# An expert layer whose slots fetch their own token rows: an indirect gather beside each indirect return

## The chip, the cores and the metric

The kernel runs on one core of one Trainium2 chip. The metric is the device time of one execution in microseconds (us). Before the change it is 2861.53 us, the median of three runs that lie between 2859.42 and 2862.87 us.

## The reference, cut to what matters

The kernel computes a nonlocal block, an attention layer with three branches, and a layer of eight experts, over 4 x 1024 tokens of 128 channels. Only the last layer is touched:

```python
m = jnp.mean(x, -1); xn = (x - m) / sqrt(var + eps)   # layer norm of 4096 tokens x 128
logits = xn @ router_w.T                              # 8 experts
probs = softmax(logits); p2, i2 = top_k(probs, 2)     # two experts a token
p2 = p2 / (sum(p2) + 1e-9)
h = silu(xn @ w1[e].T) * (xn @ w3[e].T)               # 341 hidden units
y = h @ w2[e].T                                       # back to 128 channels
out = x + sum over the two chosen e of p2[e] * y[e]
```

The 4096 tokens give 8192 pairs of token and expert. Pairs are sorted by expert into slots of 128 rows. Each expert is padded to whole slots, so that 64 + 7 = 71 slots always suffice.

## The kernel before, in words

Three stages run one behind the other, each closed by a barrier of all engines: the heads, the attention, and the experts (`experts_part`). The last has two blocks with a barrier between them.

`route_block` loads the tokens, turns them (PE, L1569; ACT, L1594), normalizes them into `xe[0]` (DVE, L1648), turns them back for the router (PE, L1577; ACT, L1602), multiplies by the router (PE, L1582) and takes softmax, ranks and the position of each pair among the slots (DVE, L1653 to L1704). Meanwhile SP clears the 9088 rows of `xs` in DRAM (L1555): each row has 128 values and one word, the number of the pair, which starts out of range. POOL makes a second copy `xe[1]` of the rows (L1620). When `where` is there (L1704), POOL issues 64 indirect DMAs (L1627), two for each tile of 128 tokens, which scatter the rows with their pair numbers to their places in `xs`. It waits until all have landed. DVE works out the gates and the owner (the expert) of each slot (L1707 to L1713). ACT rounds the three weight tensors to a high part (L1607, L1608), and DVE subtracts it to get the low part (L1716, L1719).

`experts_block` runs over the 71 slots. SP loads groups of `GROUP` = 4 slots from `xs` into one of three buffers of `xin` (L1764). A load waits for the returns of the group that had the buffer before. PE runs, in step i: `hidden(i)` (six matmuls, L1802 to L1807); in every fourth step, where i % 4 is 1, `turn_x(i // 4 + 1)`, four transposes of the next group (L1789); then `turn_h(i - 1)` (L1816) and `output(i - 2)` (L1826, L1828). ACT and DVE follow in the same order: silu, split of x and of h, and `result(i - 2)`, a copy and an addition into one of four buffers `y` (L1924, L1926). For each slot POOL waits for that result and issues one indirect DMA (L1894) that returns the 128 rows to their places in `ys`; the row numbers are the word beside each row of `xin`. At the end SP loads `ys` in order (L1773), DVE adds with the gates, and PE, ACT and SP turn and store.

All instructions of an engine run in the order of the code. A wait stands in that order and holds all that is behind it.

Of the kernel before, what the change touches and what calls it, by code (L numbers as in the profile page):

```python
# [8 lines left out]
F32 = mybir.dt.float32  # L9
# [6 lines left out]
P = 128  # L16
# [1464 lines left out]
ROW = P + 1  # L1481
GROUP = 4
LAST_ROWS = HIDP - (KH - 1) * P
# [3 lines left out]
def experts_part(nc, d, t2_dram, out, ps, ident, eps, sb, kept):  # L1487

    m = Mem()
    m.ps, m.ident, m.eps = ps, ident, eps
    m.xs = kept("xs", (SLOTS * P, ROW))
    m.ys = kept("ys", (2 * B * T, C))
    m.w1 = [sb(n, [C, NE, HIDP], F32R) for n in ("w1h", "w1l")]
    m.w3 = [sb(n, [C, NE, HIDP], F32R) for n in ("w3h", "w3l")]
    m.w2 = sb("w2hl", [P, NE, KH, 2, C], F32R)
    m.t_tok = sb("t_tok", [P, TILES_OF, P])
    m.gate = sb("gate_of", [P, 2, TILES_OF])  # L1500
    m.owner = sb("owner", [P, SLOTS], I32)
    with ExitStack() as mem:
        route_block(nc, m, d, t2_dram, lambda *a: mem.enter_context(nc.sbuf_tensor(*a)))
    experts_block(nc, m, out, sb)


def route_block(nc, m, d, t2_dram, sb):
# [3 lines left out]
    raw = [sb(n, [P, x], F32) for n, x in (("raw_w1", NE * HIDP), ("raw_w3", NE * HIDP), ("raw_w2", NE * KH * C))]  # L1511
    t2 = sb("t2_all", [C, B, T], F32)
    xe = [sb("xe%d" % k, [P, TILES_OF, ROW], F32) for k in range(2)]
    xf = t2[:].rearrange("c b t -> c (b t)")
    empty = sb("empty", [P, ROW], F32)
# [4 lines left out]
    token = sb("token", [P, 2, TILES_OF], I32)  # L1520
# [12 lines left out]
    slot = sb("slot", [P, 2, TILES_OF], F32)  # L1533
    where = sb("where", [P, 2, TILES_OF], I32)
    owner_f = sb("owner_f", [P, SLOTS], F32)
    stack = ExitStack()
    s = open_sems(nc, stack, "w_loaded t_loaded0 t_loaded1 t_loaded2 t_loaded3 small_loaded empty_set cleared w_hi "
                             "turned t_copied stats aggregated std_done xn_done back back_copied logits_done shifted "
                             "exp_done chosen_done counted placed scattered chain id_done copied ones_set")
# [3 lines left out]
    with nc.Block() as block:  # L1543
        @block.sync
        def _(sp):
            for b in range(B):
                sp.dma_start(t2[:, b, :], t2_dram[b]).then_inc(s["t_loaded%d" % b], 16)
            small = ((router, "router"), (tie, "tie"), (before, "before"), (token, "token"), (steps, "steps"),
                     (places, "places"))
            for dst, name in small:  # L1550
                sp.dma_start(dst[:], d[name]).then_inc(s["small_loaded"], 16)
            for k, name in enumerate(("w1", "w3", "w2")):
                sp.dma_start(raw[k][:], d[name]).then_inc(s["w_loaded"], 16)
            sp.wait_ge(s["empty_set"], 2)
            sp.dma_start(m.xs.rearrange("(i p) n -> p i n", p=P),  # L1555
                         empty[:].unsqueeze(1).to_broadcast([P, SLOTS, ROW])).then_inc(s["cleared"], 16)
            sp.wait_ge(s["cleared"], 16)
# [4 lines left out]
        def _(pe):  # L1562
# [9 lines left out]
            for g in range(groups):  # L1572
# [3 lines left out]
                for i in range(GROUP):  # L1576
                    mm = pe.transpose(ps[:, 2 + g % 2, i * P:(i + 1) * P], xe[0][:, GROUP * g + i, 0:P], m.ident[:])  # L1577
                mm.then_inc(s["back"], 1)
            pe.wait_ge(s["small_loaded"], 16 * 6)
            for t in range(TILES_OF):  # L1580
# [7 lines left out]
                .then_inc(s["counted"], 1)  # L1588

        @block.scalar  # L1590
        def _(act):
# [13 lines left out]
            act.wait_ge(s["w_loaded"], 48)  # L1605
            for k, (hi, lo) in enumerate((m.w1, m.w3)):
                act.copy(hi[:].rearrange("p e n -> p (e n)"), raw[k][:]).then_inc(s["w_hi"], 1)  # L1607
            act.copy(m.w2[:, :, :, 0, :], raw[2][:].rearrange("p (e k n) -> p e k n", e=NE, k=KH)).then_inc(s["w_hi"], 1)  # L1608

        @block.gpsimd  # L1610
        def _(pool):
            pool.memset(empty[:, 0:P], 0.0).then_inc(s["empty_set"], 1)
            pool.memset(empty[:, P:ROW].bitcast(I32), 2 * B * T).then_inc(s["empty_set"], 1)
            pool.wait_ge(s["small_loaded"], 16 * 6)
            for k in range(2):
                pool.tensor_copy(xe[k][:, :, P].bitcast(I32), token[:, k, :]).then_inc(s["id_done"], 1)
            for g in range(groups):
                gg = slice(GROUP * g, GROUP * (g + 1))
                pool.wait_ge(s["xn_done"], GROUP * (g + 1))
                pool.tensor_copy(xe[1][:, gg, 0:P], xe[0][:, gg, 0:P]).then_inc(s["copied"], 1)  # L1620
            pool.wait_ge(s["cleared"], 16)
            pool.wait_ge(s["id_done"], 2)
            pool.wait_ge(s["copied"], groups)
            pool.wait_ge(s["placed"], 1)
            for t in range(TILES_OF):
                for k in range(2):
                    pool.indirect_dma_start(m.xs, bass.IndirectOffsetOnAxis(ap=where[:, k, t:t + 1], axis=0),  # L1627
                                            xe[k][:, t, :], None, bounds_check=SLOTS * P - 1, oob_is_err=False)\
                        .then_inc(s["scattered"], 16)
            pool.wait_ge(s["scattered"], 16 * PAIRS_OF)  # L1630

        @block.vector
        def _(dve):
# [9 lines left out]
            for b in range(B):  # L1643
# [3 lines left out]
                for t in range(NT * b, NT * (b + 1)):  # L1647
                    dve.tensor_scalar(xe[0][:, t, 0:P], m.t_tok[:, t, :], mv[:, t, 0:1], rstd[:, t:t + 1], ALU.subtract,  # L1648
# [16 lines left out]
            dve.wait_ge(s["small_loaded"], 16 * 6)  # L1665
# [35 lines left out]
            for k in range(2):  # L1701
                run(dve.tensor_tensor(picked[k], chosen[:, k], pos[:], ALU.mult))
                run(dve.tensor_reduce(slot[:, k, :], picked[k], AX, ALU.add))
            dve.tensor_copy(where[:], slot[:]).then_inc(s["placed"], 1)  # L1704
# [9 lines left out]
            for k, (hi, lo) in enumerate((m.w1, m.w3)):  # L1714
                dve.wait_ge(s["w_hi"], k + 1)
                dve.tensor_tensor(lo[:].rearrange("p e n -> p (e n)"), raw[k][:],  # L1716
                                  hi[:].rearrange("p e n -> p (e n)").bitcast(F32), ALU.subtract)
            dve.wait_ge(s["w_hi"], 3)
            dve.tensor_tensor(m.w2[:, :, :, 1, :], raw[2][:].rearrange("p (e k n) -> p e k n", e=NE, k=KH),  # L1719
                              m.w2[:, :, :, 0, :].bitcast(F32), ALU.subtract)  # L1720
# [4 lines left out]
def experts_block(nc, m, out, sb):  # L1725
# [4 lines left out]
    m.xin = sb("xin", [P, 3, GROUP, ROW])  # L1730
# [6 lines left out]
    m.y = sb("y_out", [P, 4, C])  # L1737
# [5 lines left out]
                             "hi_done lo_done y_ready y_done put0 put1 put2 put3 got0 got1 got2 got3 got4 got5 got6 got7 half_done added out_ready "  # L1743
# [6 lines left out]

    def puts_before(i, k):

        return len(range(k, i, 4))

    with nc.Block() as block:
        @block.sync
        def _(sp):
            for g in range(loads):
                if g >= 3:
                    last = tiles(g - 3)[-1]  # L1760
                    for k in range(4):
                        sp.wait_ge(s["put%d" % k], 16 * puts_before(last + 1, k))
                n = len(tiles(g))
                sp.dma_start(m.xin[:, g % 3, 0:n, :],  # L1764
                             m.xs[GROUP * g * P:(GROUP * g + n) * P].rearrange("(i p) n -> p i n", p=P))\
                    .then_inc(s["in%d" % (g % 3)], 16)
            for k in range(4):
# [15 lines left out]
        def _(pe):  # L1783
            def turn_x(g):
                pe.wait_ge(s["in%d" % (g % 3)], 16 * (g // 3 + 1))
                if g > 0:
                    pe.wait_ge(s["xl_done"], g)
                for i in range(len(tiles(g))):
                    mm = pe.transpose(ps[:, 7, i * P:(i + 1) * P], m.xin[:, g % 3, i, 0:P], m.ident[:])  # L1789
# [99 lines left out]
        def _(pool):  # L1889
            for i in range(SLOTS):  # L1890
                g = i // GROUP
# [133 lines left out]
```

## Time and profile before

| | |
|---|---|
| median of three runs | 2861.53 us |
| profiled execution, its own time | 2860.51 us |
| its span, first to last instruction | 2858.6 us |
| PE busy over the span | 2337.6 us (82%) |
| DVE busy | 1682.3 us (59%) |
| ACT busy | 1215.4 us (43%) |
| POOL busy | 537.8 us (19%) |
| route block, about | 2473 to 2636 us |
| experts block, about | 2636 to 2858 us |

How to read it: the stages follow one another, so that the busy shares of the whole span say little of this change. It lies wholly behind 2473 us, and there each stage has another engine that works. The page also has the span in 40 slices of 71.5 us each, in which PE is busy for 2 tenths of slice 36 and for less than one of slice 37. DMA records give the time from issue to landing. The granted clock is the clock at which TensorE was let run, in shares of 2.4 GHz: 0.50 is 1.2 GHz and 1.00 is 2.4 GHz. A time in brackets behind an instruction is the idle time of its engine before it, and the arrow names what ended it.

### The profile page before, as it was taken

What the parts mean: (1) busy time and instruction counts of PE and PEld (TensorE: products, weight loads), DVE (VectorE), ACT (ScalarE), POOL (GpSimd) and SP (SyncE); (2) the same over time, 40 slices, a digit from 0 to 9 for tenths busy, and PEclk for the clock granted to TensorE, in tenths of its full rate; (3) what the DMA queues carried; (4) which work ended last, traced back from release to release, by engine and by line L of the source; (5) the groups of instructions that cost most, each with busy time, mean ns of one, the idle gap of its engine ahead of it and who ended that gap; (6) DMA issues with size and microseconds to landing.
All of it is one profiled execution on the core that took longest, in us unless ns stands there. A gap on an engine that the chain in (4) does not pass through costs nothing. (4 is left out here: it accounts for less than half of the span.)

```text
span 2858.6 us, 46600 instructions
## 1 busy us (share of the span) xinstructions
PE 2337.6 (82%) x16656; PEld 1554.2 (54%) x16656; DVE 1682.3 (59%) x3155; ACT 1215.4 (43%) x2665; POOL 537.8 (19%) x575
## 2 busy tenths in 40 slices
PE   5585867763899999799999799999899999620995
PEld 3354545542566666466566466666566665310884
DVE  4767676764366566366566365665465664550676
ACT  2343333430455555355455355555355555410442
POOL 0133333352011011011011010110010110235332
PEclk8787887885999999899999899999899999755997
DMA  2254545478647546455655465565466461431113
GB/s 94 99 212 164 189 182 196 171 284 204 138 96 145 126 97 138 106 126 109 127 125 119 91 132 125 114 130 117 105 139 125 97 145 37 127 58 52 46 52 108
DMA packets 222862, 360.74 MB, mean 126 GB/s; under 512 B 68794, under 2 KB 124701, under 8 KB 222240
## 3 DMA queue, kind: packets, MB, share of 16 engines
q1 hardware_dynamic: 218304, 349.20, 48.8%
q0 software_dynamic: 4320, 8.43, 0.9%
q8 instruction: 141, 2.31, 0.4%
q14 instruction: 97, 0.79, 0.1%
HBM read 229.58 MB, written 126.56 MB: 125 GB/s over the span
## 5 line engine op out<-in xcount | busy, mean ns | idle before, releaser
L1400 ACT ACTIVATE prob<-ps 128x512 f32<-128x512 f32 (+5 forms) x1600 | 636.5, 441 | 733.5 <-PE ps L1351 587.7
L1453 DVE TENSOR_REDUCE maxima<-ps 128x1 f32<-128x512 f32 (+3 forms) x768 | 387.7, 547 | 293.7 <-PE ps L1279 146.5
L1372 PE MATMUL ps<-prob,plain 128*32 128x512 f32 (+5 forms) x3200 | 512.0, 443 | 0.0
L1423 POOL TENSOR_TENSOR products<-products,sums 128x256 f32<-128x256 f32 x192 | 140.3, 731 | 1604.5 <-DVE sums L1444 1603.2
L1458 DVE TENSOR_REDUCE maxima<-ps 128x2 f32<-128x512 f32 (+1 forms) x512 | 294.2, 608 | 242.9 <-PE ps L1290 99.7
L1444 DVE RECIPROCAL sums<-sums 128x256 f32<-128x256 f32 x192 | 331.5, 1736 | 103.9 <-ACT sums L1411 103.9
L1343 PE MATMUL ps<-q1a_s,k1a_s 128*128 128x512 f32 (+3 forms) x768 | 303.4, 395 | 0.0
L1351 PE MATMUL ps<-q1b_s,k1b_s 128*128 128x512 f32 (+3 forms) x768 | 301.3, 393 | 0.0
L1372 PE MATMUL ps<-prob,v_s 128*32 128x512 f32 (+3 forms) x1536 | 284.4, 491 | 0.0
L1279 PE MATMUL ps<-k1a_s,q1a_s 128*128 128x512 f32 (+3 forms) x768 | 234.4, 375 | 2.8 <-DMA k1a_s<-k1ah_dram 2.8
L1343 PEld LDWEIGHTS ps<-q1a_s,k1a_s 128*128 128x128 f32 x768 | 147.4, 192 | 126.8 <-issue 118.9
L1409 ACT ACTIVATE products<-ps,gates_a 64x512 f32<-64x512 f32 x192 | 131.0, 682 | 194.6 <-PE ps L1372 194.5
L1343 PE MATMUL ps<-qa_s,kwa_s 128*128 128x192 f32 (+2 forms) x576 | 175.2, 304 | 19.5 <-ACT prob L1400 15.9
L1351 PE MATMUL ps<-qb_s,kwb_s 128*128 128x192 f32 (+2 forms) x576 | 184.2, 323 | 0.0
L1343 PEld LDWEIGHTS ps<-qa_s,kwa_s 128*128 128x128 f32 x576 | 110.0, 191 | 98.2 <-issue 65.6
L932 POOL TENSOR_TENSOR rope<-turned 128x512 f32<-128x512 f32 (+1 forms) x80 | 93.5, 1168 | 353.5 <-DVE turned L959 350.5
L1279 PEld LDWEIGHTS ps<-k1a_s,q1a_s 128*128 128x128 f32 x768 | 145.8, 197 | 20.8 <-DVE maxima L1453 8.1
L1351 PEld LDWEIGHTS ps<-q1b_s,k1b_s 128*128 128x128 f32 x768 | 151.7, 198 | 5.4
L1298 PE MATMUL ps<-kwa_s,qa_s 128*128 128x192 f32 x512 | 124.8, 326 | 33.9 <-DMA kwa_s<-kwh_dram 33.9
L1372 PEld LDWEIGHTS ps<-prob,plain 128*32 128x32 f32 x3200 | 147.7, 109 | 0.0
L914 ACT CAST pairs<-ps 128x512 fp32r<-128x512 f32 (+1 forms) x112 | 62.2, 555 | 197.5 <-PE ps L888 115.8
L1343 PE MATMUL ps<-qa_s,ksa_s 128*128 128x512 f32 x256 | 114.2, 446 | 37.3 <-issue 18.9
(332 smaller groups left out, 4837.1 us busy)
## 6 DMA issues: line engine op xcount, KB each, us to landing
qh_dram<-pairs SPq DMA_DIRECT2D x96, 512.0 KB, 3.3
kwh_dram<-pairs SPq DMA_DIRECT2D x64, 512.0 KB, 3.0
qa_s<-qh_dram SPq DMA_DIRECT2D x128, 256.0 KB, 4.5
kwa_s<-kwh_dram SPq DMA_DIRECT2D x128, 256.0 KB, 7.4
q1a_s<-qh_dram SPq DMA_DIRECT2D x128, 256.0 KB, 4.7
qb_s<-qh_dram SPq DMA_DIRECT2D x64, 256.0 KB, 9.0
kwb_s<-kwh_dram SPq DMA_DIRECT2D x64, 256.0 KB, 9.9
k1a_s<-k1ah_dram SPq DMA_DIRECT2D x32, 512.0 KB, 6.9
```

The source lines that it names most:

```text
L932: pool.tensor_tensor(m.rope[:, j % 2, 0:w], m.turned[:, j % 2, 0, 0:w], m.turned[:, j % 2, 1, 0:w], ALU.add).then_inc(s["added"], 1)
L1279: mm = pe.matmul(bank[:, 0:k1 - k0], m.q1a[:, k, h, i * P:(i + 1) * P], m.k1a[:, k, k0:k1], start=True, stop=True)
L1298: pe.matmul(bank[:, i * KEEP:i * KEEP + WN], m.qa[:, k, h, t * P:(t + 1) * P], m.kwa[:, k, h, k0:k0 + WN], start=True, stop=True, skip_gro ...
L1343: pe.matmul(bank, kx, qx[:, k, h, q0:q0 + w], start=True, stop=False, skip_group_check=True)
L1351: pe.matmul(bank, ky, qy[:, k, h, q0:q0 + w], start=False, stop=True, skip_group_check=True)\
L1372: mm = pe.matmul(ps[at:at + VD, SCORES + k % 2, q0 - c * CH:q0 - c * CH + w], w_, m.prob[:, n % PROBS, h, 0:w], start=first, stop=True, sk ...
L1400: act.activation(m.prob[:, u % PROBS, h, 0:w], ps[:, turn % SCORES, 0:w], ACT.Exp, scale=SCALE).then_inc(s["exp_done"], 1)
L1409: act.activation(m.products[rows, br, cc], ps[0:NW, SCORES + k % 2, :], ACT.Copy, scale=m.gates[0:NW, br:br + 1])
L1423: pool.tensor_tensor(o, o, m.sums[:, br, cc], ALU.mult).then_inc(s["divided"], 1)
L1444: dve.reciprocal(total, total).then_inc(s["inverse_done"], 1)
L1453: ins = dve.tensor_reduce(partial[:, h, i, part:part + 1], bank[:, 0:w], AX, ALU.max)
L1458: ins = dve.tensor_reduce(negs[1 if kind == "max1" else 2][:, at:at + 2], bank.rearrange("p (i n) -> p i n", i=2)[:, :, 0:w], AX, ALU.max, ...
```

## The change

- `xs` now holds the 4096 normalized rows in token order. SP stores them in eight DMAs of 256 KB as they get ready. The clearing, the second copy `xe[1]` and the 64 scatters are gone.
- The inverse of the placement (which pair lies in lane p of slot s) is computed. For 64 tiles of pairs, DVE makes a bf16 one-hot matrix of the lane of each pair (`at_lane`, four parts of 128x2048 elements) and a mask of the slot edges behind it (`marks`, 128x4608 elements, once compared and once multiplied by the tile's number; ACT makes a copy scaled by the token's lane). PE multiplies 64 times, one-hot (128x128) by marks (128x144), and sums in one bank. DVE turns the sums into `get` (row to fetch) and `put` (row to return to) with ten small operations.
- The high parts of w1 and w3 are rounded by ACT in the midst of its copies back, behind groups 1 and 3. The low parts are subtracted on POOL, no longer on DVE.
- In the experts block SP loads no rows. POOL fetches each slot with an indirect DMA (`get`), eight before the loop and then one ahead of each return. There are eight `y` buffers instead of four. The load of a group counts as landed when all its slots have.

```diff
-    m.xs = kept("xs", (SLOTS * P, ROW))
+    m.xs = kept("xs", (B * T, P))
@@ route_block, PE
+            for q in range(QUARTERS):
+                pe.wait_ge(s["lanes_done"], q + 1)
+                pe.wait_ge(s["behind_done"], 2)
+                pe.wait_ge(s["named_done"], 1)
+                for n in range(q * PAIRS_OF // QUARTERS, (q + 1) * PAIRS_OF // QUARTERS):
+                    mm = pe.matmul(ps[:, 7, 0:2 * EDGES], at_lane[:, n, :], marks[:, n].rearrange("p a s -> p (a s)"),
+                                   start=n == 0, stop=n == PAIRS_OF - 1)
+            mm.then_inc(s["found_done"], 1)
@@ route_block, ACT
                 act.copy(xf[:, g * CH:(g + 1) * CH], ps[:, 2 + g % 2, :]).then_inc(s["back_copied"], 1)
+                if g == 1:
+                    act.wait_ge(s["w_loaded"], 48)
+                if g in (1, 3):
+                    k = g // 2
+                    act.copy((m.w1, m.w3)[k][0][:].rearrange("p e n -> p (e n)"), raw[k]).then_inc(s["w_hi"], 1)
@@ route_block, POOL
-            for t in range(TILES_OF):
-                for k in range(2):
-                    pool.indirect_dma_start(m.xs, bass.IndirectOffsetOnAxis(ap=where[:, k, t:t + 1], axis=0),
-                                            xe[k][:, t, :], None, bounds_check=SLOTS * P - 1, oob_is_err=False)\
-                        .then_inc(s["scattered"], 16)
-            pool.wait_ge(s["scattered"], 16 * PAIRS_OF)
+            for k, (hi, lo) in enumerate((m.w1, m.w3)):
+                pool.wait_ge(s["w_hi"], k + 1)
+                pool.tensor_tensor(lo[:].rearrange("p e n -> p (e n)"), raw[k],
+                                   hi[:].rearrange("p e n -> p (e n)").bitcast(F32), ALU.subtract).then_inc(s["w_lo"], 1)
+            pool.wait_ge(s["w_hi"], 3)
+            pool.tensor_tensor(m.w2[:, :, :, 1, :], raw[2].rearrange("p (e k n) -> p e k n", e=NE, k=KH),
+                               m.w2[:, :, :, 0, :].bitcast(F32), ALU.subtract).then_inc(s["w_lo"], 1)
@@ route_block, DVE, in place of the cast to where
+            run(dve.tensor_copy(slot_i[:], slot[:]))
+            run(dve.tensor_scalar(lane_i[:], slot_i[:], P - 1, None, ALU.bitwise_and))
+            run(dve.tensor_copy(lane[:], lane_i[:]))
+            dve.wait_ge(s["w_lo"], 2)
+            dve.tensor_tensor(marks[:, :, 0, :], each_tile(slot[:], EDGES), each_token(edges[:], PAIRS_OF), ALU.is_ge)\
+                .then_inc(s["behind_done"], 1)
+            n = PAIRS_OF // QUARTERS
+            for q in range(QUARTERS):
+                qq = slice(q * n, (q + 1) * n)
+                dve.tensor_tensor(at_lane[:, qq, :], each_tile(lane[:, qq], P), each_token(lanes[:], n), ALU.is_equal)\
+                    .then_inc(s["lanes_done"], 1)
+                if q == 0:
+                    dve.wait_ge(s["named_done"], 1)
+                    dve.tensor_tensor(marks[:, :, 0, :], marks[:, :, 0, :], each_tile(token[:, 0:PAIRS_OF], EDGES), ALU.mult)\
+                        .then_inc(s["behind_done"], 1)
@@ experts_block, SP
-            for g in range(loads):
-                if g >= 3:
-                    last = tiles(g - 3)[-1]
-                    for k in range(4):
-                        sp.wait_ge(s["put%d" % k], 16 * puts_before(last + 1, k))
-                n = len(tiles(g))
-                sp.dma_start(m.xin[:, g % 3, 0:n, :],
-                             m.xs[GROUP * g * P:(GROUP * g + n) * P].rearrange("(i p) n -> p i n", p=P))\
-                    .then_inc(s["in%d" % (g % 3)], 16)
@@ experts_block, PE
             def turn_x(g):
-                pe.wait_ge(s["in%d" % (g % 3)], 16 * (g // 3 + 1))
+                pe.wait_ge(s["in%d" % (g % 3)], 16 * rows_in(g))
@@ experts_block, POOL
+            def get(i):
+                g = i // GROUP
+                if g >= 3 and i % GROUP == 0:
+                    pool.wait_ge(s["x_ready"], g - 2)
+                at = bass.IndirectOffsetOnAxis(ap=m.get[:, i:i + 1], axis=0)
+                pool.indirect_dma_start(m.xin[:, g % 3, i % GROUP, :], None, m.xs, at, bounds_check=B * T - 1, oob_is_err=False)\
+                    .then_inc(s["in%d" % (g % 3)], 16)
+            ahead = 2 * GROUP
+            for i in range(ahead):
+                get(i)
             for i in range(SLOTS):
-                g = i // GROUP
+                if i + ahead < SLOTS:
+                    get(i + ahead)
                 pool.wait_ge(s["y_done"], i + 1)
-                at = bass.IndirectOffsetOnAxis(ap=m.xin[:, g % 3, i % GROUP, P:ROW].bitcast(I32), axis=0)
-                pool.indirect_dma_start(m.ys, at, m.y[:, i % 4, :], None, bounds_check=2 * B * T - 1, oob_is_err=False)\
-                    .then_inc(s["put%d" % (i % 4)], 16)
+                at = bass.IndirectOffsetOnAxis(ap=m.put[:, i:i + 1], axis=0)
+                pool.indirect_dma_start(m.ys, at, m.y[:, i % Y_RING, :], None, bounds_check=2 * B * T - 1, oob_is_err=False)\
+                    .then_inc(s["put%d" % (i % Y_RING)], 16)
```

## Rows read from the trace of the kernel before

**Rows 1.** Windows by stage: busy us (count) of PE, PEld, DVE, ACT, POOL; clock; DMA

```profile
2540.00:2633.00 93.00, 0.00 (x0) 0.00 (x0) 12.46 (x10) 0.00 (x0) 67.99 (x64) 0.50 0.14 46
2650.00:2828.00 178.00, 158.35 (x1095) 142.99 (x1093) 122.31 (x362) 75.47 (x222) 69.13 (x71) 1.00 0.16 47
```

**Rows 2.** Timeline of POOL, scatters: start, us, engine, line, operation [idle before]

```profile
2550.59 2.96 POOL L1627 DMA_INDIRECT xs_dram<-xe,where  x1 [0.30 <-issue]
2553.86 0.97 POOL L1627 DMA_INDIRECT xs_dram<-xe,where  x1 [0.30 <-issue]
```

**Rows 3.** POOL's drain at the block's end; first transpose and load of the experts block

```profile
L1543 POOLq DRAIN  x1: 5280/5280/5280, 2629.4 to 2629.4; - x1
...
2635.99 1.48 SPq L1764 DMA_DIRECT2D xin<-xs_dram  x3
...
2638.94 1.12 PE L1789 MATMUL ps<-ident,xin 128*128 128x128 f32 x4 [107.04 <-DMA xin<-xs_dram]
```

**Rows 4.** Timeline of DVE in the route block

```profile
2516.65 2.29 DVE L1663 TENSOR_TENSOR more<-pr 128x2048 f32<-128x2048 f32 x1
...
2539.42 0.20 DVE L1704 CAST where<-slot 128x64 int32<-128x64 f32 x1
...
2543.46 3.05 DVE L1716 TENSOR_TENSOR w1l<-raw_w,w1h 128x2736 fp32r<-128x2736 f32 x1
```

**Rows 5.** Timeline of ACT; landing time of the largest weight load (KB, us)

```profile
2492.01 0.58 ACT L1602 COPY t_all<-ps 128x512 f32<-128x512 f32 x1 [0.73 <-PE ps L1577]
...
2515.23 2.46 ACT L1607 CAST w1h<-raw_w 128x2736 fp32r<-128x2736 f32 x1
...
raw_w<-in_w SPq DMA_DIRECT2D x1, 1536.0 KB, 14.1
```

**Rows 6.** Timeline of PE: the router's matmuls

```profile
2500.29 13.66 PE L1582 MATMUL ps<-router,t_all 128*128 128x8 f32 x64
```

**Rows 7.** Groups by line and form, POOL with two inputs: busy us, mean ns

```profile
L923 POOL TENSOR_TENSOR scr<-arena,scr 128x1024 fp32r<-128x1024 f32 x4 | 9.4, 2340 | 0.0
```

**Rows 8.** Timelines of DVE, PE and POOL over one group of four slots

```profile
2704.89 0.29 DVE L1926 TENSOR_TENSOR y_out<-ps,y_out 128x128 f32<-128x128 f32 x1
2705.67 0.60 PE L1789 MATMUL ps<-ident,xin 128*128 128x128 f32 x4
2705.95 0.97 POOL L1894 DMA_INDIRECT ys_dram<-y_out,xin  x1 [0.98 <-DVE y_out L1926]
2709.43 0.97 POOL L1894 DMA_INDIRECT ys_dram<-y_out,xin  x1 [2.51 <-DVE y_out L1926]
2711.23 0.97 POOL L1894 DMA_INDIRECT ys_dram<-y_out,xin  x1 [0.82 <-DVE y_out L1926]
2714.08 0.98 POOL L1894 DMA_INDIRECT ys_dram<-y_out,xin  x1 [1.88 <-DVE y_out L1926]
2715.80 0.60 PE L1789 MATMUL ps<-ident,xin 128*128 128x128 f32 x4
2716.10 0.97 POOL L1894 DMA_INDIRECT ys_dram<-y_out,xin  x1 [1.04 <-DVE y_out L1926]
```

**Rows 9.** The tile y_out: times from issue to landing of its 71 returns

```profile
DMA to landing us min/median/max: 2.1/2.3/3.8
```

**Rows 10.** PE behind waits; granted clock (third number from the end) after them

```profile
219.67 2.07 PE L468 MATMUL ps<-arena,wo 64*128 64x512 f32 x2 [3.97 <-DVE arena L568]
...
219.70:225.50 5.80, 5.80 (x16) 3.81 (x17) 4.04 (x7) 2.02 (x4) 1.28 (x1) 0.50 0.00 1
...
249.40 1.96 PE L617 MATMUL ps<-ident,arena 128*112 128x128 f32 x8 [3.25 <-DVE arena L701]
...
249.40:252.80 3.40, 3.40 (x12) 3.08 (x13) 0.00 (x0) 1.14 (x3) 0.00 (x0) 0.50 0.00 0
```

**Rows 11.** Timeline of PE, a slot's six matmuls at half clock and what follows

```profile
2643.42 0.49 PE L1802 MATMUL ps<-w1h,xh_t 128*128 x1
2645.12 0.81 PE L1789 MATMUL ps<-ident,xin 128*128 128x128 f32 x4
```

More of the change, by code:

```diff
@@ L1501, in experts_part @@
     m.owner = sb("owner", [P, SLOTS], I32)
+    m.get = sb("get_row", [P, SLOTS], I32)
+    m.put = sb("put_row", [P, SLOTS], I32)
     with ExitStack() as mem:
@@ L1552, in _ @@
             for k, name in enumerate(("w1", "w3", "w2")):
[L1553 to L1557, printed above, removed]
+                sp.dma_start(raw[k], d[name]).then_inc(s["w_loaded"], 16)
+            for g in range(groups):
+                sp.wait_ge(s["xn_done"], GROUP * (g + 1))
+                rows = m.xs[GROUP * g * P:GROUP * (g + 1) * P]
+                sp.dma_start(rows.rearrange("(t p) n -> p t n", p=P), xn[:, GROUP * g:GROUP * (g + 1), :])\
+                    .then_inc(s["kept"], 16)
+            sp.wait_ge(s["kept"], 16 * groups)
             sp.wait_ge(s["w_loaded"], 48)
@@ L1606, in _ @@
-            for k, (hi, lo) in enumerate((m.w1, m.w3)):
-                act.copy(hi[:].rearrange("p e n -> p (e n)"), raw[k][:]).then_inc(s["w_hi"], 1)
-            act.copy(m.w2[:, :, :, 0, :], raw[2][:].rearrange("p (e k n) -> p e k n", e=NE, k=KH)).then_inc(s["w_hi"], 1)
+            act.copy(m.w2[:, :, :, 0, :], raw[2].rearrange("p (e k n) -> p e k n", e=NE, k=KH)).then_inc(s["w_hi"], 1)
+            act.wait_ge(s["behind_done"], 1)
+            act.activation(marks[:, :, 1, :], marks[:, :, 0, :], ACT.Copy, scale=token[:, PAIRS_OF:PAIRS_OF + 1])\
+                .then_inc(s["named_done"], 1)
@@ L1713, in _ @@
             run(dve.tensor_copy(m.owner[:], owner_f[:]))
[L1714 to L1720, printed above, removed]
+            dve.wait_ge(s["found_done"], 1)
+            run(dve.tensor_copy(found[:], ps[:, 7, 0:2 * EDGES].rearrange("p (a s) -> p a s", a=2)))
+            run(dve.tensor_scalar(found[:, 0, :], found[:, 0, :], float(P), None, ALU.mult))
+            run(dve.tensor_tensor(found[:, 0, :], found[:, 0, :], found[:, 1, :], ALU.add))
+            run(dve.tensor_tensor(place_of[:], found[:, 0, 0:SLOTS], found[:, 0, 1:EDGES], ALU.subtract))
+            run(dve.tensor_scalar(spare[:], place_of[:], 0.0, float(2 * B * T + P), ALU.is_equal, ALU.mult))
+            run(dve.tensor_scalar(place_of[:], place_of[:], -float(P), None, ALU.add))
+            run(dve.tensor_tensor(m.put[:], place_of[:], spare[:], ALU.add))
+            run(dve.tensor_scalar(spare[:], place_of[:], float(B * T), -float(B * T), ALU.is_ge, ALU.mult))
+            run(dve.tensor_tensor(place_of[:], place_of[:], spare[:], ALU.add))
+            dve.tensor_scalar(m.get[:], place_of[:], 0.0, None, ALU.max)
     phase_end(nc, s)
@@ L1729, in experts_block @@
     loads = -(-SLOTS // GROUP)
-    m.xin = sb("xin", [P, 3, GROUP, ROW])
+    m.xin = sb("xin", [P, 3, GROUP, P])
     m.xh = sb("xh_t", [C, 2, CH], F32R)
@@ L1749, in tiles, with rows_in @@
         return range(GROUP * g, min(GROUP * (g + 1), SLOTS))
+    def rows_in(g):
+        return sum(len(tiles(x)) for x in range(g % 3, g + 1, 3))
     def puts_before(i, k):
-        return len(range(k, i, 4))
+        return len(range(k, i, Y_RING))
     with nc.Block() as block:
```

77 lines of the change are left out of this document (37 added, 40 removed).

## The prediction, as it was written before the result was known

> **What bounds the kernel now.** I read the stages first, then one engine at a time in the stages that the diff touches. Everything ahead of 2473 us is untouched. In the route block the end is set by POOL: between 2540 and 2633 us PE and ACT do nothing, while POOL works through 64 scatters [rows 1]. One takes 0.97 us and 0.30 us go by before the next, so 1.28 us each, some 82 us, and 87 with four that are stretched [rows 2]. Behind them come the landing and a drain of 5.3 us, and then the barrier: the experts block's first load is issued at 2635.99 and its first transpose, `turn_x(0)`, runs at 2638.94 [rows 3]. In the experts block PE is the bound: 158 of 178 us busy at the full clock, with POOL busy for 69 [rows 1]. A group of four slots takes 2715.80 - 2705.67 = 10.13 us from one `turn_x` to the next [rows 8]. So the change is worth what it moves `turn_x(0)` forward, less what it adds to the 71 slots.
>
> **Route block, up to the placement.** SP's eight stores run beside other work, and nobody on the path waits for them; the clearing, which kept SP busy but not the path, costs nothing to lose. On ACT two casts of 2.46 us [rows 5] are put ahead of copies on which PE's last transposes wait. Group 1 is copied at 2492.6; the largest weight load took 14.1 us with the clearing beside it, which puts its landing near 2494 [rows 5], so ACT may wait up to 1.6 us there. Followed through the order (copy 0.6 us each, four transposes 1.1 us, a transpose of group g behind the copy of g - 2), the router's matmuls begin near 2503.2 and not at 2500.3 [rows 6]: +2.9 us, between 1.4 if the weights are early and 4. The low parts go to POOL: 2.34 us for 1024 elements with two inputs [rows 7], so some 6 us each for w1 and w3, done by 2509, while DVE asks for them only near 2543: hidden. The third starts near 2521, beside DVE's long operations; POOL's instruction was stretched from 0.97 to 2.96 us beside such ones [rows 2], so 6.5 us may become 20 and end at 2541, far ahead of the block's end.
>
> That stretch is what the Trainium skill states in GPSIMD Engine Reference, section 1: POOL's SBUF interface is shared with VectorE, with contention when a DVE instruction has two SBUF inputs. By that rule nearly all the new DVE work (mask and one-hot compares) could hold POOL's third subtraction; even held until DVE's last compare and then run for 6.5 us, it would move the block's end by 1 us at most.
>
> **Route block, the inverse placement.** The slots are known at 2539.4 + 2.9 = 2542.3 [rows 4]. DVE takes 2.29 us for 2048 elements [rows 4], so about 1.05 ns an element and 0.15 fixed. Three small operations, 0.7 us; the compare of 4608 elements, 5.0, until 2548.0. ACT's scaled copy of 4608 elements costs 4.1 at the 0.9 ns of its cast [rows 5] and ends at 2552.2; DVE makes the first one-hot part meanwhile (2.3) and waits 1.9. The product of 4608, 5.0, until 2557.2. Three more one-hot parts, 6.9, until 2564.1; gates and owner follow, 3.9 as between 2539.5 and 2543.46 [rows 4], until 2568. PE's 64 products start at 2557.2. No row shows a bf16 product of 144 columns at half clock. The nearest, f32 with 8 columns, is 13.66 / 64 = 0.21 us [rows 6]; bounds are 0.12 (then DVE's last part sets it: 2566) and 0.33 (2578). I take 0.23 with some of them at full clock: 2569. Ten small operations, 2.5 us: 2571.6. The barrier, from POOL's drain at 2634.7 to 2635.99, took 1.3 [rows 3]; this time POOL has no indirect DMA to drain. POOL then starts at 2573.3 with 0.4 for its own start.
>
> **Start of the slots.** `turn_x(0)` needs four gathers. No row shows an indirect gather. I price it as the return of the same 64 KB: 0.97 us of POOL, 1.28 in a row [rows 2], landed 2.3 us after its start [rows 9]. Bounds are 0.6 and 1.6 us of POOL, and 1.5 and 2.9 to land, the last being what SP's first load took, 2635.99 to 2638.94 [rows 3]. So 2573.3 + 3.84 + 2.3 = 2579.5 against 2638.94: **-59.4 us**, between -66 and -50.
>
> The skill's DMA: Bandwidth & Descriptors (Anatomy of one DMA, SWDGE path) gives about 2.0 us and bytes / 436e3 a DMA, an estimate of 2.15 us for 64 KB, and says that most of it is the receipt of the write, heaviest when the target is HBM. The returns, which write HBM, agree (2.3); a gather writes SBUF and so might land sooner. With 2.15 in place of 2.3 the sum below would be some 2.5 us lower.
>
> **The slots.** The new order on POOL is: get(i + 8), wait for result i, put(i). So get(4g + 3), the last row set of group g, stands behind put(4g - 6), and that waits for result 4g - 6. PE computes `output(4g - 6)` in step 4g - 4, and wants `turn_x(g)` in step 4g - 3, behind one `hidden`. Before, SP's load of a group waited only for the returns of the group three before it. Now one `hidden` must cover result, put, get and landing; it can't. In the rows: DVE has the result at 2705.18, POOL starts the put at 2705.95, 0.77 later, and PE wants `turn_x` at 2705.67 [rows 8]. The four returns of a group start 3.76, 5.56, 8.41 and 10.43 us behind its `turn_x` [rows 8]. With a get of 1.28 behind each, POOL runs 3.76, 6.32, 8.88, 11.44; the last get starts at 12.72, lands at 15.02, and the next `turn_x` is at 15.07: **+4.94 us a group**. POOL's queue makes 1.0 of that, the latency the rest. Behind the waiting `turn_x` stand `turn_h` and `output`, so that no other work fills the gap. The eight `y` buffers don't help: results wait for no return today, and what is late is the get, not the buffer.
>
> The idle time has a second price. After waits of 3.97 and 3.25 us on PE, the granted clock is 0.50 for 5.8 and 3.4 us [rows 10]. A stall of 4 to 5 us in each group should do the same each time; I take 5 us at half clock behind each. There six matmuls take 1.70 us and not 1.05 [rows 8, 11], and transposes and outputs grow likewise, so that a slot is bound by PE at about 3.9 us instead of 2.5. In 5 us that costs 0.5 for the four transposes and 1.5 for the rest: 2.0. The third return may then start at 10.41, the last at 12.97 (behind POOL's get), the get at 14.25, `turn_x` at 16.60: **+6.47 a group**.
>
> Sum over `turn_x(1)` to the end: `turn_x(1)` has its rows in time (gets 4 to 7 end before PE's start-up does). `turn_x(2)`: +4.4. Groups 3 to 16: 14 x 6.47 = 90.6. The last group has three slots, its last get stands behind the third return: +3.9, and 2.0 of half clock behind it. Together **+100.9**. The tail (gather of `ys`, addition, store) is unchanged.
>
> 2860.5 - 59.4 + 100.9 = 2902.0 for the profiled execution, which stood 1.0 below the median of the runs: 2903.
>
> **Rivals.** (a) The stall is there, the clock stays high, as it did over all the slots before [rows 1]: +4.4 + 14 x 4.94 + 2.4 = 76.0, so 2860.5 - 59.4 + 76.0 + 1.0 = 2878. Against it stand [rows 10]. 20%. (b) The other side: the gather is short. What decides is the time from DVE's result to landed rows: I have 0.77 + 0.97 + 0.31 + 2.3 = 4.35 and 1.0 of queue. The gain of 59.4 over 15.5 groups pays for 3.8 us a group; with 0.5 us of POOL and 1.2 to land the stall is 2.8, and if the clock stays up too: 2861 - 59.4 + 43 = 2845. With no stall at all only POOL's pace is left, 142 x 1.28 = 182 us against 178: 2806. For it speaks that no row shows a gather; against, that both kinds of scatter took 0.97. 10%, of which 8 are faster and 2 within 0.2%. (c) The gather is dear: 1.6 us of POOL and 2.9 to land add 1.3 to 1.9 a group, and 3 at the start: 2925 to 2935. 10%. Main case 60%, between 2885 and 2918.
>
> **How the numbers follow.** Most likely 2903. The range reaches down to case (a) with an early start and up to most of (c): 2865 to 2930. About 0.2% is what a measurement of this kernel can tell from no change; beyond it: faster 0.08, same 0.03, slower 0.89.
>
> **What would show it.** `turn_x(0)` near 2580. PE's waits for `xin` at L1789 sixteen times, 4 to 5 us each, ended by a DMA from `xs`, with groups 15 to 17 us long (the step on dependency). The granted clock at 0.5 behind each (case a: at 1.0). POOL at 1.28 a DMA. A gather of under 0.7 us on POOL that lands within 1.5 would make the prediction wrong, and so would a one-hot stage that ends before 2560 or after 2585.

## The result, and the profile after

The changed kernel takes 2916.68 us (median; 2915.18 to 2920.9), the kernel before 2860.48 us beside it: the ratio is 1.0199, 95% interval [1.0185, 1.0214]. So it is slower by 2.0%. The forecast was 2903 us and slower. The profiled execution took 2917.1 us (span 2915.3 us), against 2860.51 us (span 2858.6 us) before.

The page's line of busy times:

```profile
PE 2376.2 (82%) x16720; PEld 1593.2 (55%) x16720; DVE 1700.0 (58%) x3170; ACT 1221.0 (42%) x2666; POOL 558.7 (19%) x573
```

The windows by stage (busy us and count of PE, PEld, DVE, ACT, POOL; granted clock; DMA share; GB/s):

```profile
2520.00:2577.00 57.00, 8.05 (x68) 6.34 (x68) 50.97 (x63) 4.25 (x2) 7.41 (x1) 0.56 0.00 0
2600.00:2850.00 250.00, 162.22 (x917) 150.64 (x916) 103.26 (x302) 65.18 (x186) 117.57 (x116) 0.79 0.11 31
2700.00:2750.00 50.00, 32.50 (x188) 30.14 (x186) 20.73 (x60) 13.63 (x39) 23.52 (x24) 0.80 0.11 30
```

The share of 82% is the same as before and says nothing; the windows do. The route block's end belongs to DVE now (50.97 of 57 us), no longer to POOL [rows 1]. In the slots PE is busy for only 65% of the time, at a clock of 0.79; before it was busy for 158 of 178 us at 1.00 [rows 1]. No engine is full there: the slots are bound by latency.

The waits of PE from 2580 us on (us in total, times, longest):

```profile
PE ps L1817 <- DMA xin<-xs_dram,get_row: 101.2, 17, 13.9
```

The first of the 17 is the start of the block; the sixteen others are `turn_x(2)` to `turn_x(17)`, which wait for their gathered rows for 3.6 to 7.9 us each. Before, `turn_x` (L1789) had one wait for its rows in the slots, of 0.57 us.

Spans put the difference of 56.7 us together. `turn_x(0)` moved from 2638.94 to 2584.51: -54.4. From there to `turn_x(17)` it is 277.7 us and not 168.9: +108.8. The rest up to the end went from 50.8 to 53.1: +2.3.

One group in the changed kernel, the rows of L1817 (PE), L1923 (a gather) and L1934 (a return) in the timeline:

```profile
2705.04 1.02 POOL L1923 DMA_INDIRECT xin<-xs_dram,get_row  x1 [0.30 <-issue]
2708.39 1.11 PE L1817 MATMUL ps<-ident,xin 128*128 128x128 f32 x4 [6.18 <-DMA xin<-xs_dram,get_row]
2712.76 1.01 POOL L1934 DMA_INDIRECT ys_dram<-y_out,put_row  x1 [6.70 <-DVE y_out L1966]
2714.08 1.03 POOL L1923 DMA_INDIRECT xin<-xs_dram,get_row  x1 [0.30 <-issue]
2715.86 1.01 POOL L1934 DMA_INDIRECT ys_dram<-y_out,put_row  x1 [0.75 <-issue]
2717.18 1.03 POOL L1923 DMA_INDIRECT xin<-xs_dram,get_row  x1 [0.30 <-issue]
2718.51 1.02 POOL L1934 DMA_INDIRECT ys_dram<-y_out,put_row  x1 [0.30 <-issue]
2719.83 1.03 POOL L1923 DMA_INDIRECT xin<-xs_dram,get_row  x1 [0.30 <-issue]
2721.16 1.02 POOL L1934 DMA_INDIRECT ys_dram<-y_out,put_row  x1 [0.31 <-issue]
2722.49 1.03 POOL L1923 DMA_INDIRECT xin<-xs_dram,get_row  x1 [0.30 <-issue]
2725.05 1.11 PE L1817 MATMUL ps<-ident,xin 128*128 128x128 f32 x4 [5.22 <-DMA xin<-xs_dram,get_row]
```

Read it upwards. `turn_x` at 2725.05 waits for the gather at 2722.49; that stands in POOL's queue behind the return at 2721.16; and the next return comes only after that `turn_x`, since PE computes nothing while it waits. It is the loop that the prediction drew from [rows 8]: last return 12.77 us behind `turn_x` (forecast 12.97), its gather at 14.10 (14.25), the next `turn_x` at 16.66 (16.60).

The clock behind that stall, in windows of the same columns:

```profile
2708.40:2710.50 2.10, 2.10 (x10) 2.08 (x11) 0.35 (x1) 0.91 (x3) 0.00 (x0) 0.50 0.00 0
2710.50:2712.50 2.00, 2.00 (x9) 2.00 (x9) 1.43 (x5) 0.21 (x2) 0.00 (x0) 0.50 0.00 0
2714.00:2716.00 2.00, 1.97 (x15) 1.71 (x14) 1.54 (x5) 0.91 (x3) 1.17 (x2) 1.00 0.25 70
```

After an idle time of 6.18 us PE works at 1.2 GHz for 4.1 us, all of them busy, and then is at 2.4 GHz again: the pattern of [rows 10], once a group.

The route block, rows of the timeline in order of time:

```profile
2494.26 2.47 ACT L1629 CAST w1h<-raw_w 128x2736 fp32r<-128x2736 f32 x1 [3.09 <-DMA raw_w<-in_w]
2520.19 7.41 POOL L1644 TENSOR_TENSOR w2hl<-raw_w,w2hl 128x3072 fp32r<-128x3072 f32 x1 [11.47 <-ACT w2hl L1632]
2521.01 8.73 DVE L1679 TENSOR_TENSOR same<-pr 128x2048 f32<-128x2048 f32 x1
2529.78 2.29 DVE L1681 TENSOR_TENSOR same<-same,tie 128x2048 f32<-128x2048 f32 x1
2548.70 4.96 DVE L1723 TENSOR_TENSOR raw_w<-slot,edges 128x4608 bf16<-128x4608 f32 x1
2553.69 4.13 ACT L1634 ACTIVATE raw_w<-raw_w,token 128x4608 bf16<-128x4608 bf16 x1 [33.58 <-DVE raw_w L1723]
2557.86 4.96 DVE L1732 TENSOR_TENSOR raw_w<-raw_w,token 128x4608 bf16<-128x4608 bf16 x1 [2.00 <-ACT raw_w L1634]
2562.92 3.71 PE L1608 MATMUL ps<-raw_w,t_all 128*128 128x144 bf16 x32 [22.43 <-DVE raw_w L1732]
2569.48 1.17 PE L1608 MATMUL ps<-raw_w,t_all 128*128 128x144 bf16 x16 [1.03 <-DVE t_all L1728]
2575.52 0.20 DVE L1753 TENSOR_SCALAR get_row<-place_of 128x71 int32<-128x71 f32 x1
2577.84 1.21 POOL L1923 DMA_INDIRECT xin<-xs_dram,get_row  x1 [50.24 <-POOLq L46]
2584.51 1.12 PE L1817 MATMUL ps<-ident,xin 128*128 128x128 f32 x4 [13.86 <-DMA xin<-xs_dram,get_row]
```

The third row is the surprise: a DVE operation of the kind that takes 2.29 us [rows 4], and does so again in the fourth row, took 8.73 us while POOL subtracted the low part of w2.

### The profile page after: what moved, and what is told of

It is laid out like the page before. It is cut to its first block and busy times, and to the rows that moved or that the text cites. A ratio compares the mean times of both kernels' runs of the same rounds, so it can differ in the third digit from the quotient of the medians.

```text
span 2915.3 us, 46714 instructions
## 1 busy us (share of the span) xinstructions
PE 2376.2 (82%) x16720; PEld 1593.2 (55%) x16720; DVE 1700.0 (58%) x3170; ACT 1221.0 (42%) x2666; POOL 558.7 (19%) x573
```

## The experiments

Times are medians beside the kernel before in the same session. "Group" is the mean time between one `turn_x` and the next over groups 3 to 16, in the profiled execution: 10.20 us before, 17.20 us in the changed kernel. "Late silu" counts ACT's activation of a slot (L1892 in the changed kernel) where it starts more than 0.4 us after the slot's own matmul, for which it waits, has ended and ACT is free: 0 of 71 before, 15 of 71 (14.4 us together) in the changed kernel.

**1. Is it the distance of the gathers?**

```diff
-            ahead = 2 * GROUP
+            ahead = 3 * GROUP
```

> The changed kernel with gathers twelve slots ahead of the returns instead of eight (three groups, which three buffers can hold), nothing else. My theory, that the stall is the chain from a result over a return and a gather to the landed rows, gives each gather 4 slots (10 us) more time: no waits for xin at turn_x after the first, granted clock 1.00 over the slots, experts block back to the 219.7 us from turn_x(0) to the end, so 2916.7 - 111 = 2806 us (2800 to 2815 for POOL's pace of 1.33 us a DMA). Rival: POOL's pace is the bound, with two indirect DMAs a slot whatever their distance; then 71 x 2.65 = 188 us and waits remain; together with the start, 2820 to 2830. Rival: contention between gathers and returns slows both: over 2850.

Measured: 2858.84 us, ratio 0.9987 [0.9973, 1.0]. No `turn_x` behind the first waits for rows any more, and 58 us are gained. So the loop of return, gather and `turn_x` is what made the change slow: one number undoes it. But 2806 us was expected, and the groups stay at 13.47 us, irregular between 10.5 and 16.2. What PE and ACT wait for now, from 2585 us on (us in total, times, longest; "remote" is a wait that was ended by an update of a semaphore with no instruction of the profile ending at that time):

```profile
PE ps L1854 <- DVE y_out L1966: 31.5, 17, 3.4
ACT act_s L1892 <- remote: 22.4, 12, 3.3
```

Late silus: 22, 28.6 us together. The expectation's third rival, contention between gathers and returns, had over 2850 us, which fits the time. Something new holds the slots; runs 7 to 12 look for it.

**2. The eight result buffers**

```diff
-Y_RING = 8
+Y_RING = 4
```

> The changed kernel with four y buffers as before the change, not eight. My theory: results never wait for returns, so 2917 within 0.2%. Rival: a return now lands later, behind gathers on the same queue, and four buffers hold DVE back: over 2925.

Measured: 2920.12 us, ratio 1.0202 [1.0185, 1.0219], against 1.0199 [1.0185, 1.0214] with eight: no difference that can be told. The four added buffers buy nothing, as results wait for no return.

**3. The collision of w2's subtraction with DVE**

```diff
+            act.copy(m.w2[:, :, :, 0, :], raw[2].rearrange("p (e k n) -> p e k n", e=NE, k=KH)).then_inc(s["w_hi"], 1)
             act.wait_ge(s["shifted"], 1)
             ...
-            act.copy(m.w2[:, :, :, 0, :], raw[2].rearrange("p (e k n) -> p e k n", e=NE, k=KH)).then_inc(s["w_hi"], 1)
```

> The changed kernel, with ACT's rounding of w2 moved ahead of the softmax's exponential, so that POOL's third subtraction falls into 2509 to 2516, where DVE waits for the router. Theory: the 8.73 us of DVE's operation at 2521 (2.29 in the kernel before) is POOL's 7.41 us subtraction with two SBUF inputs holding DVE; moved, the operation takes 2.3 again and the kernel loses 6.4 us: 2910. Rival: the long operation has another cause (a stall in its data or in the shared interface that stays): 2917.

The cast goes ahead of ACT's wait for the softmax, so that POOL subtracts before DVE's compares begin. The two rows in that run:

```profile
2508.60 6.69 POOL L1644 TENSOR_TENSOR w2hl<-raw_w,w2hl 128x3072 fp32r<-128x3072 f32 x1
2520.94 2.28 DVE L1679 TENSOR_TENSOR same<-pr 128x2048 f32<-128x2048 f32 x1
```

The collision is shown: 8.73 us becomes 2.28, and `turn_x(0)` is at 2578.06, 6.45 us sooner. The changed kernel and the ten runs of this study without the edit all have 8.73 or 8.74; the two with it (this and the next) have 2.28. Yet the time is 2917.82 us, ratio 1.0184 [1.0167, 1.0202], an interval that overlaps the changed kernel's: no gain of 6.4 us can be told. In the profiled execution (2920.66 us) the groups grew to 17.89 us; one wait for rows came to 8.74 us:

```profile
2637.12 1.12 PE L1817 MATMUL ps<-ident,xin 128*128 128x128 f32 x4 [8.74 <-DMA xin<-xs_dram,get_row]
```

**4. Both edits**

> Both at once, gathers twelve ahead and w2 rounded early. If the two costs are independent, 2806 - 6.4 = 2799 to 2800 us, 2.1% under the kernel before. If POOL's pace sets the slots, an earlier start moves it all the same: e1 less 6.4.

The diffs of 1 and 3 together. Measured: 2854.63 us, ratio 0.9978 [0.9967, 0.999]. It is the best complete version found: 4.2 us below run 1, near the second expectation (run 1 less 6.4) and far from the first, and 0.2% faster than before.

**5 and 6. The price of the half clock**

```diff
             def turn_x(g):
-                pe.wait_ge(s["in%d" % (g % 3)], 16 * rows_in(g))
                 if g > 0:
                     pe.wait_ge(s["xl_done"], g)
+                for _ in range(36 if g >= 2 else 0):
+                    pe.matmul(ps[:, 7, 0:P], m.ident[:], m.ident[:], start=True, stop=True)
+                pe.wait_ge(s["in%d" % (g % 3)], 16 * rows_in(g))
```

> The changed kernel, with 36 idle matmuls of 128 columns (their result is overwritten) on PE ahead of each wait for rows from turn_x(2) on: about 0.11 us each at the full clock, 4.1 us, inside the stall of 5.3. The chain of returns and gathers is as it was. My theory: the stall has a second price, the half clock behind it; with PE kept busy the clock stays at 1.00, and each group of 17.1 us gets near my 15.07 + 0.3: 16 x 1.7 = 27 us less, 2890 (2885 to 2897). Rival: the clock costs nothing, since the next stall takes up what it costs: 2917. If the clock falls all the same, the idle matmuls take twice as long and push past the landing: over 2935.

Measured: 2936.53 us, ratio 1.0257 [1.0228, 1.0286]. The run missed its aim: one such matmul takes some 0.22 us and not the 0.11 I had put, so that 36 of them outlast the stall and lengthen the groups to 18.21 us themselves. The same with `range(18 ...)`:

> The changed kernel with 18 matmuls of the identity by itself (128x128, f32) ahead of the wait for the rows in turn_x, for groups 2 to 17; in the run with 36 of them one took about 0.22 us and they outlasted the stall. 18 take 4.0 us and so lie inside a stall of 5 to 6. Their result is overwritten by the transposes. Theory (half the clock behind each stall costs 2.0 us a group): the clock stays at 1.00, waits for xin shrink to 1 or 2 us, groups 15.2 us instead of 17.2, 2886 us in all. Rival (the clock costs nothing, what lengthens the group is the stall alone): 2917, as the changed kernel. Rival (late starts take back part of it): 2895 to 2908.

Measured: 2923.33 us, ratio 1.0228 [1.021, 1.0245]. A window of some three groups, with the columns as above:

```profile
2700.00:2760.00 60.00, 50.73 (x369) 47.64 (x368) 26.45 (x78) 16.17 (x48) 29.65 (x29) 0.97 0.11 32
```

A `turn_x` in the timeline of that run, with the wait that is left:

```profile
2640.93 0.66 PE L1819 MATMUL ps<-ident,xin 128*128 128x128 f32 x4 [2.25 <-DMA xin<-xs_dram,get_row]
```

The clock is up (0.97, and 0.93 from 2640 to 2760 us, against 0.80), `turn_x` takes 0.66 us where it took 1.11, and still the groups take 17.56 us. Keeping the clock up gave back no time. Where the time goes stands in the starts of the returns behind their `turn_x`, medians in us over `turn_x(2)` to `turn_x(16)`:

| | clock, 2640 to 2760 us | first return | second | third | fourth |
|---|---|---|---|---|---|
| changed kernel | 0.80 | 4.38 | 7.78 | 10.43 | 13.07 |
| 18 matmuls added | 0.93 | 3.85 | 7.00 | 9.66 | 13.79 |
| 36 matmuls added | 1.00 | 3.80 | 6.45 | 9.11 | 13.82 |

Up to the third return the higher clock does give back 0.8 and 1.3 us. The fourth comes later all the same, since its result comes late (a median of 13.0 us in both runs, against 11.7): late silus rose from 14.4 us in all to 27.6 and 36.6. Whether the added matmuls themselves make more late starts isn't shown. So these runs confirm my price of 2.0 us for the half clock in part, and not in the time of a group.

**7 and 8. Distances between eight and twelve**

`ahead = 9`:

> Gathers nine ahead, one more than in the change. Theory: the last gather of a group stands one return earlier, 2.6 us, so a stall of 5.3 becomes some 2.7; with the clock falling behind it all the same, 16 x 2.65 = 42 us less: 2874. If a stall of 2.7 leaves the clock up, 1.7 less in each group: 2848. Rival (POOL's pace is the bound): POOL's work per group stays 10.6 us, below the group's time, so it can't tell here; under it nothing would be gained: 2917.

Measured: 2872.06 us, ratio 1.003 [1.0013, 1.0046]. As expected: waits of 2.1 to 3.0 us at `turn_x(2)` to `turn_x(16)` (0.4 at the last). The clock still fell to half once in each group, though not always right at the wait (`turn_x` takes 0.66 to 1.12 us); its mean from 2600 to 2800 us is 0.86. `ahead = 10`:

> Gathers ten ahead. Theory: two returns earlier, 5.3 us, as much as the stall: almost none is left (under 0.5 us a group), the clock stays up: 2806 to 2815. Rival: POOL falls behind, since two DMAs a slot take 2.65 us against PE's 2.51, and a stall comes back in the later groups: 2820 to 2840.

Measured: 2862.0 us, ratio 1.000 [0.9986, 1.0013], not 2806 to 2815. Nearly all waits for rows are gone, and the groups take 13.34 us nevertheless, with 23 late silus (27.6 us). So one step more, nine for eight, brings 45 of the 58 us that twelve bring, and from ten on the distance isn't the matter.

**9. The rows without gathers**

```diff
+            for g in range(loads):
+                if g >= 3:
+                    sp.wait_ge(s["x_ready"], g - 2)
+                n = len(tiles(g))
+                first = min(GROUP * g, TILES_OF - GROUP) * P
+                sp.dma_start(m.xin[:, g % 3, 0:n, :], m.xs[first:first + n * P].rearrange("(i p) n -> p i n", p=P))\
+                    .then_inc(s["in%d" % (g % 3)], 16)
```

with POOL's gathers taken out.

> The changed kernel with no gathers: SP loads four slots at a time straight from xs, with a wait for the buffer's last transposes alone. It leaves out the gathering: the slots get rows in token order, not those of their pairs. It says what the gathers cost in all. Theory: turn_x(0) 2.9 us behind the block's start, 3.7 earlier than with four gathers, and no stall: 2806 - 4 = 2802. Rival: the returns themselves or the new row numbers slow the slots: over 2815.

Measured: 2806.16 us, ratio 0.9807 [0.9778, 0.9836]. Groups 10.13 us, no late silu of 71. This is what run 1 had been expected to give: 52.7 us lie between gathers that nobody waits for and none at all.

**10 to 12. What of the gather costs it.** To the kernel of run 9, 63 DMAs of 64 KB are added, one a slot, on whose data nothing waits: indirect gathers into a spare buffer on POOL,

```diff
+                if i + 8 < SLOTS:
+                    if i >= 4:
+                        pool.wait_ge(s["sp%d" % (i % 4)], 16 * (i // 4))
+                    at = bass.IndirectOffsetOnAxis(ap=m.get[:, i:i + 1], axis=0)
+                    pool.indirect_dma_start(m.spare[:, i % 4, :], None, m.xs, at, bounds_check=B * T - 1, oob_is_err=False)\
+                        .then_inc(s["sp%d" % (i % 4)], 16)
                 pool.wait_ge(s["y_done"], i + 1)
```

> The kernel whose rows SP loads in token order (2806 us; the output leaves out the gathering), with 63 indirect gathers of 64 KB on POOL added, one ahead of each return, into a buffer of their own that nobody reads. PE waits for none of them. Theory (a gather issued back to back with a return makes the other engines start late): groups 12 to 14 us instead of 10.1, late starts of ACT's silu (over 0.4 us behind its matmul) in 15 or more of 71 slots against none, 2845 to 2860 us. Rival (the late starts come of the order of PE's own waits in the changed kernel, POOL only paces): groups 10.3 at most, 2806 to 2810.

indirect returns of a constant into a spare DRAM space (the same with `m.spare[i % 4], at, m.ident[:], None` and the rows of `put`),

> The kernel whose rows SP loads in token order (2806 us; the output leaves out the gathering), with 63 indirect returns of 64 KB added, one ahead of each true return, of the constant identity to a DRAM space of their own. Theory A (any second indirect DMA does it): as with added gathers, 2845 to 2860 us. Theory B (it is the gather, which reads scattered rows and writes the SBUF): no late starts, groups 10.3 at most, 2806 to 2812 us.

and plain loads into the spare buffer, issued by SP behind the same results (`sp.dma_start(m.spare[:, i % 4, :], m.xs[at:at + P])`).

> The kernel whose rows SP loads in token order (2806 us; the output leaves out the gathering), with 63 plain loads of 64 KB added, one a slot, issued by SP at the pace of the results, into a buffer of their own that nobody reads. With as many indirect DMAs added on POOL it took 2861 (gathers) and 2865 us (returns). Theory A (what costs is the indirect DMA, made by POOL): 2806 to 2812 us, groups 10.1 to 10.3, no late starts. Theory B (what costs is 64 KB more a slot in the DMA engines): 2850 to 2865 us, with late starts as there.

| added to run 9 | us | ratio to before | group, us | late silus, us together |
|---|---|---|---|---|
| nothing | 2806.16 | 0.9807 [0.9778, 0.9836] | 10.13 | 0 |
| 63 gathers, POOL | 2860.81 | 1.0001 [0.999, 1.0013] | 13.62 | 20, 31.8 |
| 63 returns, POOL | 2864.68 | 1.0017 [1.0003, 1.0032] | 13.86 | 23, 38.8 |
| 63 plain loads, SP | 2804.6 | 0.9796 [0.9781, 0.9811] | 10.13 | 0 |

The window from 2620 to 2720 us of each, first with nothing added:

```profile
2620.00:2720.00 100.00, 91.12 (x634) 82.58 (x632) 71.19 (x209) 44.21 (x130) 38.19 (x40) 1.00 0.16 51
```

With plain loads:

```profile
2620.00:2720.00 100.00, 91.21 (x634) 82.70 (x632) 70.86 (x208) 44.32 (x130) 38.37 (x40) 1.00 0.26 78
```

With gathers:

```profile
2620.00:2720.00 100.00, 78.34 (x474) 71.94 (x472) 52.33 (x155) 31.37 (x94) 60.26 (x59) 0.88 0.20 57
```

With returns:

```profile
2620.00:2720.00 100.00, 78.21 (x453) 70.27 (x452) 50.31 (x149) 30.15 (x92) 55.57 (x58) 0.86 0.17 54
```

The plain loads move the most (78 GB/s, DMA share 0.26) and PE does the same 634 matmuls as without them. With a second indirect DMA a slot, the DMA engines are less busy than that (0.20, 0.17), POOL is busy for only 60 of 100 us, nobody waits for the data, and PE does only 474 or 453. PE's clock fell to 0.88 and 0.86 there, so a part of the price may be the clock's. Traffic of that size is out as the cause, and it doesn't matter much whether the second DMA gathers or scatters. What costs 55 to 59 us, 0.9 us for each one added, is that POOL issues two indirect DMAs a slot. The runs don't part POOL's issuing from the queue: POOL's DMAs go through the software queue (q0 of the profile), the plain ones through the hardware queue (q1), and no run gave POOL other work of the same length. How a late start looks, in the run with spare gathers:

```profile
2668.95 1.00 POOL L1935 DMA_INDIRECT ys_dram<-y_out,put_row  x1 [0.31 <-issue]
2670.17 0.32 PE L1842 MATMUL ps<-w1h,xl_t 128*128 x1
2670.25 1.04 POOL L1931 DMA_INDIRECT spare_in<-xs_dram,get_row  x1 [0.30 <-issue]
2672.00 1.00 POOL L1935 DMA_INDIRECT ys_dram<-y_out,put_row  x1 [0.71 <-issue]
2672.81 0.46 ACT L1900 ACTIVATE act_s<-ps 128x342 f32<-128x342 f32 x1 [3.06 <-remote]
```

and without them:

```profile
2667.07 0.32 PE L1841 MATMUL ps<-w1h,xl_t 128*128 x1
2667.43 0.46 ACT L1899 ACTIVATE act_s<-ps 128x342 f32<-128x342 f32 x1 [0.79 <-PE ps L1841]
```

Silu needs the matmul of the second row, which ends at 2670.49; ACT is idle, and starts at 2672.81, 2.3 us late. Without the added gathers it starts 0.04 us after the end. Silu isn't alone. In the runs with spare gathers and spare returns, ACT's rounding of h starts over 0.4 us late in 9 and 13 of 71 slots, and DVE's copy of the result in 10 and 6. All three wait for matmuls of PE. Where DVE or PE waits for ACT or DVE alone, it is punctual in every run: DVE's subtraction behind ACT's rounding and DVE's addition behind its copy start at most 0.04 us late, PE's `turn_h` behind DVE at most 0.06. The trace has the time of each update of a semaphore, too. In every late silu of every run, an update of the semaphore of PE's matmul is recorded 0.02 us ahead of the start, and so it is for all 71 silus of the kernel before, of run 9 and of the run with plain loads (in the other runs some updates of punctual silus have no record). So ACT isn't slow to start: the news that PE's matmul is done comes late. The ends of matmuls are modelled in the profile, so it doesn't tell whether the matmul itself or its signal is late, and why that happens while POOL issues two indirect DMAs a slot isn't settled. In all 29 late silus of the two runs up to 2740 us two indirect DMAs had started within 2.8 us ahead of the moment from which silu could have run, but so they had in 39 of the 62 that weren't late. No run changed the spacing alone, nor the number of rows of a DMA.

## Why the prediction was right, and where it was off

**Direction and mechanism: right, and shown.** The stall chain (return, gather behind it in POOL's queue, landing, `turn_x`) stands in the rows above within 0.2 us at each link, and run 1 cuts it with one number.

**Route block: 54.4 us gained, 59.4 forecast.** The router began at 2502.44, 0.8 sooner than forecast. The term that failed is the price of the third subtraction, "so 6.5 us may become 20": I let only POOL pay. POOL was hardly slowed (7.41 against 6.69 us alone) and DVE was held for 6.45 us; run 3 shows it. The rule that the Trainium skill gives in GPSIMD Engine Reference, section 1, that POOL shares its SBUF interfaces with VectorE, names contention and not who yields; I weighed it for POOL alone and had it move the end "by 1 us at most". By the trace it was DVE that yielded. From the mask on, everything took its price (4.96, 4.13, 4.96 us for forecasts of 5.0, 4.1, 5.0), and the products were cheap: 64 in four parts, the last 16 in 1.17 us, so 0.07 us each for the 0.23 that I took. So DVE set the end and not PE, as in the lower bound; but with its gates and owner, which the prediction itself lets end at 2568, later than the 2566 of that bound: -1.6. Barrier and start of POOL took 2.1 us and not 1.7, the four gathers to `turn_x(0)` 6.7 and not 6.1. Together -0.8 + 6.45 - 1.6 + 0.4 + 0.5 = 5.0 us.

**Slots: +111.1 us against +100.9.** `turn_x(2)` cost 5.4 (4.4), groups 3 to 16 98.0 (90.6), the last 5.4 and 2.3 behind it (3.9 and 2.0). The gather was priced right as a twin of the return: 1.02 us of POOL and 0.30 between, so 1.33 a step for 1.28, and 2.52 to 3.65 us from its start to `turn_x` for 2.35, mostly 2.6. That is 0.3 us a group. The mean group (17.20) exceeds 16.60 by 0.60. Of the other half, 0.18 is one group: from `turn_x(14)` to `turn_x(15)` it took 19.53 us, since POOL started the second return 3.20 us behind its result and not about 0.8. The rest isn't in my list of terms, and what the late starts (14.4 us in silus alone) took isn't told apart from what the half clock took. The figure of the Trainium skill for landing (DMA: Bandwidth & Descriptors, Anatomy of one DMA), 2.15 us as an estimate, was the worse guide here: the transposes that wait for a gather start mostly 2.6 us behind it, so the gathers landed hardly sooner than the returns (2.3 us, [rows 9]).

**The half clock: seen, its price confirmed in part.** That PE would be at half clock behind each stall is right (4.1 us in the group shown, 5 taken). That this costs 2.0 us a group agrees with the third and fourth return in that group (10.12 and 12.77 us behind `turn_x`; 10.41 and 12.97 forecast, 8.88 and 11.44 without a price). With the clock held up by added matmuls the third return came at 9.11 us, near the 8.88, so 1.3 us of the 1.5 that the forecast had put there go with the clock. But the fourth came late and the groups were no shorter. So rival (a), 2878 us, is out by its premise, the clock's price for a whole group stays open, and with it 24.9 us of the sum (the distance to rival (a)). The late starts weren't in the sum at all; as far as they took the place of this term, that the sum came within 14 us is luck.

**The rivals.** (b) gave 2806 us for rows that are never late, "only POOL's pace is left". Its premise was made true in run 1, and the time was 2859. This is the largest error in the text, hidden since the case didn't come about: I took two indirect DMAs a slot to cost POOL's time and nothing else. Runs 10 and 11 price what was left out at 55 to 59 us, about all that the route block gains (54.4). (c), the dear gather with 1.6 us of POOL, is refuted by 1.02 us.

## What to carry to other kernels

Before a load is moved into a queue behind a wait, count from the event that the wait needs to the landed data, and set that against the distance in steps; here one step of prefetch more (`ahead` 8 to 9) was worth 45 us and four 58. Price an indirect DMA not by the queue that issues it: two of them a slot made what waits for PE's matmuls in this kernel start late, 0.9 us for each one added, while plain DMAs of the same bytes cost nothing that could be measured, so a gather that nobody waits for can still cost as much as the scatter it replaces. Where POOL and DVE both read large tensors from SBUF, count the overlap against both.

## What the runs showed of the hardware that was not expected

- POOL's subtraction with two inputs of 3072 elements held DVE's comparison of 2048 for 8.73 us against 2.28, while POOL took 7.41 us against 6.69: DVE started 0.8 us after POOL and ended 2.1 us after it, about its own 2.28 us. Before, POOL's indirect DMA had been the one that was stretched beside DVE, 0.97 to 2.96 us [rows 2].
- With two indirect DMAs a slot on POOL, ACT started its silu up to 4.55 us (mostly 0.5 to 2.5) after the modelled end of its matmul in 15 to 23 of 71 slots (29 in run 5); with one a slot, or with plain DMAs added, in none. The update of the matmul's semaphore was late each time, and ACT followed it by 0.02 us; DVE and PE behind ACT or DVE alone were punctual. The cause is open.
- An indirect gather of 128 rows of 512 bytes takes 1.02 us of POOL, as the return does, and the transposes that wait for it start mostly 2.6 us (2.52 to 3.65) after its start; 1.33 us go by from one indirect DMA to the next.
- With waits of only 2.1 to 3.0 us, once a group (run 7), PE's clock still fell to 0.50 once in each group, as with the waits of mostly 5 to 6 us in the changed kernel (means 0.86 and 0.79).
- A bf16 product of 128x128 with 144 columns takes 0.07 us in a row of 16 at full clock; an f32 product of 128x128 with 128 columns, 0.22 us.
